# Relation products with two gathered tiles, twelve raw weight chunks and two tiles to a loop turn

## What is computed

```python
seg = edge_type * n + dst
agg = segment_sum(x[src], seg, 34 * n)
cnt = segment_sum(ones, seg, 34 * n)
mean = agg.reshape(34, n, -1) / maximum(cnt, 1).reshape(34, n, 1)
h1 = einsum('rni,rio->no', mean, W_rel) + x @ W_root + b_rgcn
xw = h1 @ W_gcn
# then a normalised sum over edges of xw[src], xw / deg, b_gcn,
# and the residual x, which is the "kept" array of the kernel
```

## Time and profile before

| | |
|---|---|
| time, median of 3 runs | 3707.63 us (3701.94 to 3717.08) |
| the profiled execution's own time | 3711.78 us |
| its span | 3709.8 us |
| granted TensorE clock over the span | 0.903 |
| PE busy | 2861.9 us, 77% |
| DVE busy | 2408.1 us, 65% |
| ACT busy | 1847.7 us, 50% |
| POOL busy | 1766.6 us, 48% |
| matmuls of the relation products (L1921) | 3264 with `wh`, 1632 with `wl` |
| loads of raw weights | 204 of 384 KB |

### The profile page before, as it was taken

The page is one execution under the profiler, slowest core; times in us unless marked ns, Lnnn a source line. Parts: engine busy times, 40 slices in busy tenths (PEclk is TensorE's granted clock), DMA queues, the critical chain, the costliest instruction groups (busy, mean ns, idle before and its releaser), DMA issues. The chain is left out here.

```text
span 3709.8 us, 60872 instructions
## 1 busy us (share of the span) xinstructions
PE 2861.9 (77%) x12846; PEld 2113.1 (57%) x12847; DVE 2408.1 (65%) x4966; ACT 1847.7 (50%) x5370; POOL 1766.6 (48%) x2269
## 2 busy tenths in 40 slices
PE   0495888888698799994566999999999934444699
PEld 0253444444355455552336999999999934444455
DVE  5233988898766888885654555555555559999312
ACT  0011888888621223221334666666656648888300
POOL 1574455554345666662113444444444457777100
PEclk9997999999899899997788999999999966666799
DMA  1334334443411555553116777777777745555300
GB/s 34 111 92 137 118 120 125 123 130 120 148 36 51 168 160 155 155 155 127 43 47 224 230 235 227 231 234 226 236 229 230 222 147 175 174 178 175 106 13 29
DMA packets 153406, 544.95 MB, mean 147 GB/s; under 512 B 34946, under 2 KB 35958, under 8 KB 153057
## 3 DMA queue, kind: packets, MB, share of 16 engines
q0 software_dynamic: 85264, 370.75, 32.2%
q1 hardware_dynamic: 46498, 123.55, 10.7%
q10 hardware_dynamic: 21600, 50.14, 4.5%
HBM read 461.05 MB, written 83.59 MB: 147 GB/s over the span
## 5 line engine op out<-in xcount | busy, mean ns | idle before, releaser
L1921 PE MATMUL pO<-wh,gT 128*128 128x384 f32 x3264 | 879.0, 342 | 41.5 <-DVE wl L1949 41.3
L1921 PEld LDWEIGHTS pO<-wh,gT 128*128 128x128 f32 x3264 | 597.9, 189 | 51.7 <-DVE wl L1949 51.7
L781 POOL DMA_INDIRECT row<-fs_d,rec x400 | 442.1, 1105 | 351.2 <-PE pA L969 185.7
L1921 PE MATMUL pO<-wl,gT 128*128 128x384 f32 x1632 | 549.8, 337 | 0.0
L487 PE MATMUL pO<-wt,hT 128*128 128x384 f32 (+1 forms) x1200 | 419.4, 511 | 41.8 <-ACT hT L1522 19.6
L1874 ACT ACTIVATE gT<-cntge 128x256 fp32r<-128x256 f32 x822 | 326.3, 415 | 112.2 <-DVE cntge L1938 52.9
L2043 PE MATMUL pC<-identb,own 128*128 128x128 bf16 x960 | 193.6, 305 | 233.5 <-ACT cntge L2024 119.2
L907 ACT ACTIVATE sj<-sj 128x96 f32<-128x96 f32 x1176 | 313.1, 268 | 99.2 <-DVE sj L1024 98.6
L487 PEld LDWEIGHTS pO<-wt,hT 128*128 128x128 f32 (+1 forms) x1200 | 236.4, 199 | 214.9 <-issue 67.8
L1935 DVE TENSOR_SCALAR cntge<-pT 128x768 int32<-128x768 int32 x137 | 131.2, 958 | 341.3 <-PE pT L480 262.2
L1921 PEld LDWEIGHTS pO<-wl,gT 128*128 128x128 f32 x1632 | 309.4, 190 | 0.0
(11 more groups left out here) (351 smaller groups left out, 5860.5 us busy)
## 6 DMA issues: line engine op xcount, KB each, us to landing
raw<-in_L_gnn_W_rel_dram SPq DMA_DIRECT2D x204, 384.0 KB
startrow<-seen_d ACTq DMA_DIRECT2D x141, 320.0 KB
row<-fs_d,rec POOLq DMA_INDIRECT x400
kept_d<-fdt ACTq DMA_DIRECT2D x1, 3840.0 KB
kept<-kept_d SPq DMA_DIRECT2D x1, 3840.0 KB
fs_d<-of SPq DMA_DIRECT2D x9, 388.0 KB, 2.5
fd_d<-of SPq DMA_DIRECT2D x9, 388.0 KB
xt<-in_x_dram SPq DMA_DIRECT2D x9, 384.0 KB
```

Of the source, the lines that this page charges most:

```text
L781: pool.indirect_dma_start(b["row"][u][:, j, :].bitcast(words), None, table, bass.IndirectOffsetOnAxis(ap=b["rec"][u][:, 2 * j + field:2 * ...
L1921: last = pe.matmul(pO[:, q, 0:HALF], gT[:, c, half, :].bitcast(F32R), w[:, c, lo:up].bitcast(F32R), start=c == 0 and k == 0, stop=c == KC ...
```

## The change

- `g` gets two halves, each with a semaphore. POOL now makes the list of tile k+2, waits for PE to have transposed tile k and issues the gather of tile k+2 into the half that came free.
- Twelve raw buffers in place of five: two relations' chunks. Ten of them are the homes of the kept rows in `fdt`, two are new. A load waits for the chunk twelve before it to have been cut, and for the load two before it to have landed, with a semaphore for the even chunks and one for the odd.
- Since the raw weights overwrite `fdt`, the kept rows must be in memory before. SP stores them tile by tile during settling, each after `kept_ok`, and ACT's one large store goes.
- Tiles of a relation are rounded up to an even number, at least four (LEAST = 4). The loops of PE and DVE take two tiles to a turn, `ctl` holds pairs, and the four instructions that evened the sum become two. The tables get RTP = 300 columns.
- The count in the second buffer runs over 1278 columns rather than 1279.

```diff
-LEAST = 2
+LEAST = 4
...
+                            for t in range(NT):
+                                kept_ok.wait(sp, 0, t)
+                                sp.dma_start(kept_d[:, t, :], fdt[:, t, 0:D]).then_inc(kept_out, 16)
+                            sp.wait_ge(kept_out, 16 * NT)
...
-                            pre.link(dve.tensor_scalar(ntiles[:], seen_keys[:, NP - 1:NP], float(P - 1), None, ALU.add))
+                            pre.link(dve.tensor_scalar(ntiles[:], seen_keys[:, NP - 1:NP], float(2 * P - 1), None, ALU.add))
...
-                            pre.link(dve.tensor_scalar(ntilesi[:], ntilesi[:], 7, None, ALU.logical_shift_right))
-                            pre.link(dve.tensor_scalar(ntiles[:], ntilesi[:], float(LEAST), None, ALU.max))
+                            pre.link(dve.tensor_scalar(ntilesi[:], ntilesi[:], 8, None, ALU.logical_shift_right))
+                            pre.link(dve.tensor_scalar(ntiles[:], ntilesi[:], LEAST / 2, 2.0, ALU.max, ALU.mult))
...
-                            pre.mark(dve.tensor_copy(ctl[0:1, C_REL:C_REL + RELS], p_ends[0:1, 0:RELS]))
+                            pre.mark(dve.tensor_scalar(ctl[0:1, C_REL:C_REL + RELS], p_ends[0:1, 0:RELS], 0.5, None, ALU.mult))
...
-                            pre.link(dve.tensor_scalar(odd[:], last_end, 1, None, ALU.bitwise_and))
-                            pre.link(dve.tensor_tensor(last_end, last_end, odd[:], ALU.add))
-                            pairs = ctl[0:1, C_PAIRS:C_PAIRS + 1]
-                            pre.link(dve.tensor_scalar(pairs, last_end, 1, None, ALU.logical_shift_right))
-                            pre.mark(dve.tensor_scalar(ctl[0:1, C_MORE:C_MORE + 1], pairs, -1.0, None, ALU.add))
+                            pre.mark(dve.tensor_copy(ctl[0:1, C_PAIRS:C_PAIRS + 1], last_end))
+                            pre.mark(dve.tensor_scalar(ctl[0:1, C_MORE:C_MORE + 1], last_end, -1.0, None, ALU.add))
...
-            COUNT = NP - 1
+            COUNT = [NP - 1, NP - 2]
...
-            g = sb("g", [P, D], F32, st)
+            g = sb("g", [P, 2, D], F32, st)
...
-            RAW = KC - 1
-            raw = [sb(f"raw{c}", [P, D], F32, st) for c in range(RAW)]
+            raw = [fdt[:, k, 0:D] for k in range(NT)] + [sb(f"raw{k}", [P, D], F32, st)[:] for k in range(2 * KC - NT)]
...
-                    def load(rel):
+                    def load(i, b):
                         for c in range(KC):
-                            if c == KC - 1:
-                                sp.wait_ge(w_ok.sem, rel * KC + 1)
-                            elif not isinstance(rel, int):
-                                sp.wait_ge(w_ok.sem, rel * KC - (KC - c - 1 if c > 0 else 0))
-                            if c == KC - 1 or not isinstance(rel, int):
+                            if not isinstance(i, int):
+                                sp.wait_ge(w_ok.sem, i * (2 * KC) + ((b - 2) * KC + c + 1))
                                 sp.sem_inc(sp_posted, 1)
-                            if c > 0 or not isinstance(rel, int):
-                                sp.wait_ge(w_in, rel * (16 * KC) + 16 * c)
-                            src = w_all[rel] if isinstance(rel, int) else w_all[ds(rel, 1)].rearrange("r p c n -> p (r c) n")
-                            sp.dma_start(raw[c % RAW][:], src[:, c, :]).then_inc(w_in, 16)
-                    load(0)
-                    with sp.Fori(1, RELS) as rel:
-                        load(rel)
-                    sp.wait_ge(w_in, 16 * KC * RELS)
+                            earlier = b * KC + c - 2
+                            if earlier >= 0 or not isinstance(i, int):
+                                sp.wait_ge(w_in[c % 2], i * (16 * KC) + 16 * (b * KC // 2 + c // 2))
+                            src = w_all[2 * i + b] if isinstance(i, int) else w_all[ds(i * 2 + b, 1)].rearrange("r p c n -> p (r c) n")
+                            sp.dma_start(raw[b * KC + c], src[:, c, :]).then_inc(w_in[c % 2], 16)
...
-                            pool.wait_ge(g_in, n * 16 + 16 * (off - 1))
+                            pool.wait_ge(g_in[b], i * 16 + 16)
...
-                        pool.indirect_dma_start(g[:], None, hr_d, bass.IndirectOffsetOnAxis(ap=gindex[b][:], axis=0))\
-                            .then_inc(g_in, 16)
+                        pool.indirect_dma_start(g[:, b, :], None, hr_d, bass.IndirectOffsetOnAxis(ap=gindex[b][:], axis=0))\
+                            .then_inc(g_in[b], 16)
...
-                    def pair(v, i, n, stores):
+                    def pair(v, i, n, out):
                         for b in range(PAIR):
+                            make_list(v, i, n, b + PAIR)
                             t_ok.wait(pool, n, b)
-                            pool.wait_ge(g_in, n * 16 + 16 * (b + 1))
                             pool.sem_inc(posted, 1)
-                            fetch((b + 1) % 2)
-                            if stores:
-                                put(v, i, n, b - PAIR)
-                            make_list(v, n, b + PAIR)
+                            fetch(b)
+                            if out is not None:
+                                put(v, out, n, b - PAIR)
                     v = Steps(pool, pool_step)
-                    make_list(v, 0, 0)
-                    make_list(v, 0, 1)
+                    make_list(v, 0, 0, 0)
                     fetch(0)
-                    pair(v, 0, 0, False)
+                    make_list(v, 0, 0, 1)
+                    fetch(1)
+                    pair(v, 0, 0, None)
...
-                    act.dma_start(kept_d, fdt[:, 0:NT, 0:D]).then_inc(kept_out, 16)
...
-                    def turn(n, off):
-                        pe.wait_ge(g_in, n * 16 + 16 * (off + 1))
+                    def turn(m, n, off):
+                        pe.wait_ge(g_in[off % 2], m * 16 + 16 * (off // 2 + 1))
                         cut_ok.wait(pe, n, off - 1)
-                        pe_transpose(pe, pT, g, P).then_inc(t_ok.sem, 1)
-
-                    turn(0, 0)
+                        pe_transpose(pe, pT, g[:, off % 2, :], P).then_inc(t_ok.sem, 1)
+
+                    turn(0, 0, 0)
                     with pe.Fori(0, RELS // 2) as i:
                         for b in range(2):
                             first, end = ends(pe, i, b)
                             w_ok.wait(pe, i, b, 1)
                             pe.sem_inc(pe_posted, 1)
-                            with pe.Fori(first, end) as n:
-                                turn(n, 1)
-                                for q, lo, up in HB:
-                                    evac_ok.wait(pe, n, -1, q + 1)
-                                    for c in range(KC):
+                            with pe.Fori(first, end) as m:
+                                n = m * PAIR
+                                for t in range(PAIR):
+                                    turn(m, n, t + 1)
+                                    for q, lo, up in HB:
+                                        evac_ok.wait(pe, n, t - 1, q + 1)
+                                        for c in range(KC):
+                                            if q == 0:
+                                                gT_ok.wait(pe, n, t, c + 1)
+                                                if t == 0:
+                                                    w_ok.wait(pe, i, b, c + 1)
+                                            for k, (half, w) in enumerate(((0, wh[b]), (0, wl[b]), (1, wh[b]))):
+                                                last = pe.matmul(pO[:, q, 0:HALF], gT[:, c, half, :].bitcast(F32R),
...
-                            dve.wait_ge(w_in, i * (32 * KC) + 16 * (off * KC + c + 1))
-                            dve.tensor_copy(wh[b][:, c, :].bitcast(F32R), raw[c % RAW][:]).then_inc(w_first, 1)
+                            dve.wait_ge(w_in[c % 2], i * (16 * KC) + 16 * (off * KC // 2 + c // 2 + 1))
+                            dve.tensor_copy(wh[b][:, c, :].bitcast(F32R), raw[b * KC + c]).then_inc(w_first, 1)
                             dve.wait_ge(w_first, i * (2 * KC) + (off * KC + c + 1))
-                            dve.tensor_tensor(wl[b][:, c, :].bitcast(F32R), raw[c % RAW][:], wh[b][:, c, :],
+                            dve.tensor_tensor(wl[b][:, c, :].bitcast(F32R), raw[b * KC + c], wh[b][:, c, :],
                                               ALU.subtract).then_inc(w_ok.sem, 1)
...
-                        with dve.Fori(first, end - 1) as n:
-                            cut_rows(n, 1)
+                        with dve.Fori(first, end - 1) as m:
+                            for t in range(PAIR):
+                                cut_rows(m * PAIR, t + 1)
+                        cut_rows(end * PAIR, -1)
                         if more:
                             cut_weights(i, b + 1, range(KC // 2))
-                        cut_rows(end, 0)
+                        cut_rows(end * PAIR, 0)
```

(10 more changed lines are left out.)

55 lines of the change are left out of this document (25 added, 30 removed).

## The result

| | before | after |
|---|---|---|
| median | 3712.36 us (3701.94 to 3720.46, 4 runs) | 3663.39 us (3660.05 to 3664.87, 4 runs) |
| profiled execution, span | 3711.78, 3709.8 us | 3660.05, 3658.2 us |
| products' stage, from SP's first load to the last product | 1039.8 us | 989.9 us |

The ratio is 0.9867 with a 95% interval from 0.985 to 0.9883. That is 49 us, inside the range on record, but two thirds of the 72 us of its sum, and outside 3616 to 3652, which the forecast's own case allowed: only the part of the range that a rival had added holds it. The stage accounts for 49.9 of the 51.7 us between the two profiled executions.

A forecast was written before the change was run, and what follows sets the result against it. The prediction took PE, with 60.8 us of waits, to bound the relation products. From 3711.8 us it took 60 and 13, added 0.6, reached 3639.4, and forecast a median of 3635 us; range 3614 to 3666.

The forecast's parts named there:

- the forecast's own case: Whole kernel: all terms come as summed, forecast 3635 us, range 3616 to 3652 us, chance 0.76.
- PE is the bound, and 60.8 us of waits can be won.: Relation products: PE bounds them, and 60.8 us of the 976.1 us window are waits.
- Weights twelve deep: Raw weight loads, two in flight: PE's 41.3 us of waits for `wl` go in every relation.
- Gathers two deep: Gathers in the products' loop, issued 13.9 us ahead instead of 6.9: PE's other 9.5 us of waits for `g` go.
- That list needs a count that ACT made a tile earlier: POOL's list, moved ahead of its wait for PE: the added wait is over when reached, charged at nothing.
- What is late next is PE itself.: Products' loop: once the wait for weight loads goes, PE is the next to be late; no size of its own.
- The start: 13 us.: Start of the products' stage: first count 10.5 us sooner, POOL's gather 2.7 us sooner; 13 us, between 11 and 15.
- Tables and stores in settling.: Wider tables cost 0.6 us (0 to 1.2); ten stores of kept rows in settling are hidden, charged at nothing.
- Even tiles change nothing.: Rounding tiles per relation to even: always four tiles already, so nothing changes; PE's register work is charged nothing.
- the 60 us: Products' loop: gain taken for deeper weights and gathers together, at least 51 and at most 61 us.
- Bursts delay the others: Rival: paired weight loads delay gathers and row loads, half of the loop's gain stays, 3665 us; chance 0.11.
- The code rival: PE's longer loop must fetch code at 50 jumps; at 5.1 us each it costs 255 us, giving 3890; chance 0.04.

The follow-up runs named there:

- put_first: The changed kernel, but POOL issues the store of products of tile k-2 ahead of the list and gather of tile k+2; ratio to before 0.9842, stage 971.5 us.
- gathers_two_deep: put_first with five raw weight buffers, one load in flight and chunk 5 in chunk 0's buffer; ratio to before 0.985, stage 972.5 us.
- weights_alone: The kernel before with only twelve raw buffers, two loads in flight and kept rows stored in settling; ratio to before 0.9888, stage 996.9 us.
- one_load: The changed kernel, but each raw load waits for the one before it, still twelve buffers; ratio to before 0.9865, stage 984.9 us.
- two_deep_list_first: gathers_two_deep with the changed kernel's order on POOL: list, gather, then store; ratio to before 0.9886, stage 985.3 us.

## Why the prediction was right, and where it was wrong

- *PE is the bound, and 60.8 us of waits can be won.* Right in the main. put_first and gathers_two_deep won 52 and 50 of the 61.7 us that the timeline has over 6.93 a tile; some 10 stayed in every kernel.
- *Weights twelve deep: the waits for `wl` go.* Right as an effect, and DVE's pace sufficed, as the earlier trace rows had it. As a cause it was too narrow. The margin of under 2 us was read rightly, but the depth isn't needed to mend it: with POOL's order mended and two gathered tiles, five homes and one load in flight do the same.
- *Gathers two deep: 9.5 us.* Right for PE's waits for `g`; but its worth is more than that, since it also keeps the loads from hurting the gathers (weights_alone).
- *"That list needs a count that ACT made a tile earlier ... so the wait added is over when reached. ... Nothing is charged for it."* **This step failed.** ACT makes that count in the same tile: it ended its read at 2209.43 + 0.19 in the changed kernel and POOL began the list at 2209.84:

```profile
2209.43 0.19 ACT L1861 ACTIVATION_READ_ACCUMULATOR acc<-startrow,after 128x1 f32 x1
```

```profile
2209.84 0.19 POOL L1791 TENSOR_SCALAR sourcef<-total 128x1 f32<-128x1 f32 x1 [0.59 <-ACT acc L1861]
...
2212.51 1.44 POOL L1797 DMA_INDIRECT g<-hr_d,gindex  x1 [0.89 <-ACT nrow L1889]
...
2215.37 1.01 POOL L1807 DMA_INDIRECT y_d<-fdt,kindex  x1 [0.82 <-POOL kindex L1806]
```

  POOL waited 200.4 us in 126 waits there. I had named what is queued behind it, the gather and the store, and priced neither. The gather could bear it (8.5 us from issue to use, where it was 5.2; the 13.9 and 6.9 of the prediction count from PE's transposes and leave out POOL's way to the issue). The store couldn't: it goes at 2215.37, and the copy that needs its landing is due some 2.7 us later (in put_first that copy starts 4.0 us after the transposes, which here are at 2214.12); it starts at 2220.68. The trace of before held the answer: the same count ends 1.35 us ahead of the store's issue (median), and the list stood behind the store, so its wait ended unseen.
- *What is late next is PE itself.* Wrong for the same reason: late next were the stores, 26.7 us of PE's time.
- *The start: 13 us.* Right. From SP's first load to the first product 34.67 became 22.06 us, 12.6 less. Up to the first transposes it is 11.8 less, and the first two tiles together take 16.1 us in both, so 11.8 reach the loop. The first count came 10.2 us sooner (10.5 taken).
- *Tables and stores in settling.* Right: six instructions over the tables went from 1.93 to 2.21 us in sum, and the stores were hidden. The line that answers to the earlier trace rows:

```profile
L1607 DVE TENSOR_SCALAR relf<-p_tile 128x300 f32<-128x300 f32 x1 | 0.5, 471 | 2.5 <-PE p_tile L1549 2.5
```

- *Even tiles change nothing.* Right in the number of tiles, but not free: a tile without a wait went from 6.93 to 6.90 us, which is 3.5 us over the stage. weights_alone, with the old loops, has 6.93; all kernels with two tiles to a turn have 6.90, and since each of them also gathers two deep, no run says which of the two does it. This gain wasn't in the sum. The register work that I had put "ahead of 6.9 us of matmuls" and charged nothing is hidden in the changed kernel; in put_first it stands where some 6 of the 9.6 us that are left there lie.
- *The sum.* 60 + 13 - 0.6 = 72.4 was forecast. Of the 51.7 measured, 34.7 are waits, 3.5 the base and 11.8 the start, which make the stage's 49.9 within rounding; 1.1 lie ahead of the stage and the rest behind it. The term that was mis-sized is the 60 us: 38.2 came. The case's own range doesn't follow from the sum either: -76 to -61 on the median of 3707.6 is 3632 to 3647, and a spread of 15 us on both sides would give 3617 to 3662 rather than 3616 to 3652. 3663 lies outside both.
- *The rivals.* "Bursts delay the others" gave 3665, nearest to the 3663 measured, but it isn't what happened: its signs, PE waiting for `g` and ACT for row loads inside the loop, are absent, and one_load took 5 us away. That the measured time lies in the range at all is luck in this sense: the range reached so far for this rival, and another mechanism of like size filled it. weights_alone, without the second gathered tile, shows the first of its signs.
- *Shared engines* (the Trainium skill, "DMA: Bandwidth & Descriptors", section "Issuing engines are not separate DMA queues"): transfers run on the same 16 engines and interleave, whichever engine issued them. What was seen agrees, without proving it: SP's loads were waited for 0.37 us less after an edit to POOL's queue alone (two_deep_list_first against gathers_two_deep), though only 0.04 less in the other such pair.
- *The code rival* didn't occur: four packets of that instruction queue in the loop, where the earlier trace rows had three, and 4.3 us of the weight load's idle time put to "issue", in one wait at the start. In put_first, with four packets too, that idle time is 15.0 us in 20 waits, and the reads of the loop bounds stand beside it.

```profile
q14 instruction: 4, 0.03, 0.0%
```

## What to carry to other kernels

When a wait is moved on an in-order queue, find when its signal really comes, in the trace, and then price everything behind it, each against its own deadline; a store has a deadline too, the next write to its buffer. Put what releases others (a store whose buffer somebody waits for) ahead of what prepares later work. And before a chain of transfers gets more buffers, look at whether a cheaper part of the change does the same: here, beside two gathered tiles, five homes of weights with one load in flight served as well as twelve with two.

## What the runs showed of the hardware that I had not expected

- The landing of a 384 KB load, one in flight on SP's queue, was waited for between 3.28 and 3.94 us on the mean, with the same bytes. The two ends are gathers_two_deep and before. Between kernels that differ only in the order of POOL's queue it moved by 0.37 us in one pair (3.65 to 3.28) and by 0.04 in another (3.51 to 3.47).
- The kernels with two tiles to a loop turn on PE and two gathered tiles take 6.90 us a tile where those with one of each take 6.93, with the same 42 matmuls.
- PE's queue took 0.303 us (median) to read a loop bound at L1751 before, 0.324 in the changed kernel and 0.875 in put_first, where only the order of POOL's issues is another than in the changed kernel.
- A scatter of 384 KB into memory, from issue to the copy that it released, took about 3.2 us when no load of weights was in flight and only a gather issued 2 us earlier (2208.23 to 2211.43 in the changed kernel), and 5.3 us beside weights, rows and gathers (2215.37 to 2220.68, and 2364.02 to 2369.35).
